# Adding the growing bank's states straight from PSUM in the down stage of a transformer layer

## The chip, the cores and the metric

The kernel runs on one core of one Trainium2 chip, in float32. The metric is the device time of one execution in microseconds (us). The engines are TensorE (PE, matmuls; PEld is its weight load), VectorE (DVE), ScalarE (ACT), GpSimd (POOL) and SyncE (SP, which issues the DMAs here). They run their own instruction streams in order and wait for one another by semaphores.

## What is computed

A layer with 2048 tokens (16 batches of 128) of width 1024: cross attention on a context, then a gated feed-forward net whose weights are 4-bit codes with scales for blocks of 64.

```python
x = x + xattn(layernorm(x), ctx, ctx)              # 8 heads
h = layernorm(x)
Wg, Wu, Wd = dequant_nf4(codes, scales)            # inner width I = 2752
inter = silu(h @ Wg.T) * (h @ Wu.T)                # 2048 x 2752
return x + inter @ Wd.T                            # 2048 x 1024: the down stage
```

## The kernel before

**Stages.** First a mixer stage (attention, up to some 180 us), then the gate and up products with the codes decoded beside them, to about 1101 us, and last the down stage, `inter @ Wd.T`, to the end. Float32 accuracy comes from splitting each operand into a high part (a cast to the matmul's rounded type) and a low part (operand less high part): each product is made of three matmuls, high by high, high by low and low by high.

**The down stage.** The inner dimension is cut into rounds of four blocks of 128 (`NR` = 5 rounds, r), the tokens into 8 pairs of tiles (`NM` = 8, m). One state g = 8r + m is one pair in one round: a 2 by 2 block product, made with 7 block products in place of 8 (the scheme of Strassen and Winograd). There are `NG` = 40 states. For a state the kernel needs the blocks of tokens themselves (`stage`, loaded by SyncE in `load_stage`, L421) and four sums S1 to S4 of them. The high parts are made by ScalarE (`hi_a`, L701, of three blocks, and `hi_s`, L707, of the four sums); VectorE makes the sums (`s_forms`, L903, four instructions of 256 columns in the tile `stemp`, shown at lines 910 and 846) and the low parts (`lo_a`, L899, 768 columns, and `lo_s`, L917, 1024 columns, both shown at line 846). The weights' forms were made in the earlier stage and are loaded once a round.

**The products of a state.** `product` (L1111) has six matmuls (128x128 by 128x512): two blocks of k, three parts each, shown at lines 1116 to 1118. The seven products 0 to 6 of a state go to three PSUM banks. Products 0, 2, 4 and 6 grow one bank, X: product 2 is accumulated onto product 0, and so on. Between them the growing sum has to be added to a part of the result. That is what the "s" adds are for: s1 takes X after product 0, s2 after product 2, s3 after product 4, and x after product 6. Products 1 and 5 grow the bank Q (adds q1 after product 1, q2 after product 5), product 3 the bank W (add w). The result `yacc` lies in SBUF with four parts of 128x512 for each pair (`part`, L932), and every add is `y = y + term` by VectorE, shown at line 930. Each finished product increments `product_done` by one, so a wait for `7g + k + 1` is a wait for product k of state g.

**How bank X is read.** ScalarE's `snapshot` (L713) copies bank X into one of two buffers `snap` as soon as the product is done (shown at line 717). TensorE waits only for that copy (`s1_ready`, `s2_ready`, `s3_ready`, L1150, L1158, L1166) and goes on with product 2, 4 or 6; VectorE adds from the copy later. The other adds, q1, q2, w and x, read PSUM directly, and TensorE waits for those of an older state or of product 1. `snap` lies over the two `inter` buffers of the stage before, so ScalarE waits for the last stores of `inter` ahead of its first copy (L735).

**The order on VectorE for a state g** (L986 to L1012): x_add(g-1), s1_add(g), s_forms(g+1), lo_a(g+1), q1_add(g), s2_add(g), w_add(g), lo_s(g+1), s3_add(g), q2_add(g). On ScalarE (L737 to L752): copy after product 0, hi_a(g+1), copy after product 2, hi_s(g+1), copy after product 4.

**The last round** (states 32 to 39) also has a rest: the inner width isn't a multiple of four blocks. After product 6 four groups of five matmuls (`rest`, lines 1125 to 1129) are added to the banks and to a bank Z, `rest_adds` (L968) takes the four adds, and a finished pair is stored. Its operands need a split too: `lo_rest` (L921) for each state, and once, in state 32, two subtractions for the weights (L1003 to L1006), all by VectorE.

Of the kernel before, what the change touches and what calls it, by code (L numbers as in the profile page):

```python
# [39 lines left out]
WIDE = 512  # L40
# [42 lines left out]
def wait(eng, sem, value):  # L83

    if not (isinstance(value, int) and value <= 0):
        eng.wait_ge(sem, value)


def xattn_ffn(nc, x, ctx, gu_codes, gu_scales, d_codes, d_scales, out):
    B, C, N = x.shape  # L90
# [8 lines left out]
    FULL = KT - 1  # L99
# [10 lines left out]
    NG = NR * NM  # L110
    KW = 4 * NR
    NP = 7
# [5 lines left out]
    with ExitStack() as st:  # L118
# [3 lines left out]
        def sem(name):  # L122
            return st.enter_context(nc.semaphore(name))
# [39 lines left out]
        def f(i, n=1):  # L163
            return F[:, i * N:(i + n) * N]
# [60 lines left out]
                 [R1[:, at_s + q * N:at_s + (q + 1) * N].rearrange("p (a n) -> p a n", a=2) for q in range(2)]]  # L225
        stage = [f(10), f(13)]
        stemp = f(11)
        snap = [F[:, 14 * N + i * WIDE:14 * N + (i + 1) * WIDE] for i in range(2)]
        blocks = [[stage[b][:, i * BK:(i + 1) * BK] for i in range(4)] for b in range(2)]
        S1, S2, S3, S4 = [stemp[:, i * BK:(i + 1) * BK] for i in range(4)]  # L230
        assert at_s + 2 * N == 2 * XW and at_a[0] + AB == 6 * ITEM
# [8 lines left out]
        bankX = [banks[0][:, 1, :], banks[3][:, 1, :]]  # L240
# [35 lines left out]
        inter_stored = [sem(f"inter_stored{s}") for s in range(2)]  # L276
# [4 lines left out]
        s_step, s_ready = sem("s_step"), sem("s_ready")  # L281
        ha_ready, la_ready, hs_ready, ls_ready = sem("ha_ready"), sem("la_ready"), sem("hs_ready"), sem("ls_ready")
        product_done = sem("product_done")
        s1_ready, s2_ready, s3_ready = sem("s1_ready"), sem("s2_ready"), sem("s3_ready")
        s1_added, s2_added, s3_added = sem("s1_added"), sem("s2_added"), sem("s3_added")
        q1_added, w_added, q2_added, x_added, z_added = [sem(n) for n in ("q1_added", "w_added", "q2_added", "x_added", "z_added")]
        restw_in, irest_in = sem("restw_in"), [sem(f"irest_in{b}") for b in range(2)]
# [298 lines left out]
        def _(act):  # L586
# [114 lines left out]
            def hi_a(g):  # L701

                act.wait_ge(stage_in[g % 2], 16 * (g // 2 + 1))
                wait(act, product_done, NP * (g - 2) + 6)
                nc.scalar.copy(aform[g % 2][0], stage[g % 2][:, 0:AB]).then_inc(ha_ready, 1)
# [4 lines left out]
                wait(act, product_done, NP * (g - 1))  # L710
                nc.scalar.copy(sform[g % 2][0], stemp.rearrange("p (a n) -> p a n", a=2)).then_inc(hs_ready, 1)

            def snapshot(g, i, product, freed, ready):  # L713

                act.wait_ge(product_done, NP * g + product + 1)
                wait(act, *freed)
                nc.scalar.copy(snap[i], bankX[g % 2]).then_inc(ready, 1)  # L717

            def hi_rest(m):

                act.wait_ge(irest_in[m % 2], 16 * (m // 2 + 1))
                wait(act, rest_done, 4 * (m - 1))
                if m == 0:
                    act.wait_ge(product_done, NP * (NG - NM))
                nc.scalar.copy(resti[m % 2][:, :, 0:2, :], irest[m % 2]).then_inc(hr_ready, 1)
# [6 lines left out]
            hi_s(0)  # L732
            last_block(2)
            last_block(3)
            for s in range(2):  # L735
                act.wait_ge(inter_stored[s], 16 * (2 * FULL + 4))
            for g in range(NG):  # L737
                r, m = g // NM, g % NM
                snapshot(g, 0, 0, (s3_added, g), s1_ready)
                if g + 1 < NG:  # L740
                    hi_a(g + 1)
                if r == NR - 1 and m == 0:
                    for k in range(2):
                        act.wait_ge(restw_in, 32)
                        nc.scalar.copy(restw[k][0], restw_in_f[k]).then_inc(hrw_ready, 1)
                    hi_rest(0)
                snapshot(g, 1, 2, (s2_added, g), s2_ready)
                if g + 1 < NG:
                    hi_s(g + 1)
                snapshot(g, 0, 4, (s1_added, g + 1), s3_ready)  # L750
                if r == NR - 1 and m + 1 < NM:
                    hi_rest(m + 1)  # L752

# [2 lines left out]
        def _(dve):  # L756
# [142 lines left out]
            def lo_a(g):  # L899
                dve.wait_ge(ha_ready, g + 1)  # L900
                sub(aform[g % 2][1], stage[g % 2][:, 0:AB], aform[g % 2][0].bitcast(F32)).then_inc(la_ready, 1)
# [15 lines left out]
            def lo_s(g):  # L917
                dve.wait_ge(hs_ready, g + 1)
                sub(sform[g % 2][1], stemp.rearrange("p (a n) -> p a n", a=2), sform[g % 2][0].bitcast(F32)).then_inc(ls_ready, 1)
# [9 lines left out]
            def add(y, term):  # L929
                return nc.vector.tensor_tensor(y, y, term, ALU.add)  # L930

            def part(g, t, h):  # L932
                return yacc[:, g % NM, t, h * WIDE:(h + 1) * WIDE]

            def s1_add(g):
                if g < NM:
                    dve.wait_ge(y_in[g], 16)
                dve.wait_ge(s1_ready, g + 1)
                add(part(g, 0, 0), snap[0]).then_inc(s1_added, 1)

            def q1_add(g):
                dve.wait_ge(product_done, NP * g + 2)
                add(part(g, 1, 1), bankQ[g % 2]).then_inc(q1_added, 1)

            def s2_add(g):
                dve.wait_ge(s2_ready, g + 1)
                add(part(g, 1, 0), snap[1]).then_inc(s2_added, 1)

            def s3_add(g):
                dve.wait_ge(s3_ready, g + 1)  # L950
                dve.wait_ge(q1_added, g + 1)
                add(part(g, 1, 1), snap[0]).then_inc(s3_added, 1)

            def w_add(g, done):
                dve.wait_ge(*done)
# [30 lines left out]
            for g in range(NG):  # L986
                r, m = g // NM, g % NM
                last = r == NR - 1
                if last and m:
                    rest_adds(g - 1)  # L990
                elif g:
                    x_add(g - 1, (product_done, NP * g))
                s1_add(g)
                if g + 1 < NG:
                    s_forms(g + 1)
                    lo_a(g + 1)
                q1_add(g)
                s2_add(g)
                if not last:
                    w_add(g, (product_done, NP * g + 4))  # L1000
                if g + 1 < NG:
                    lo_s(g + 1)
                if last and m == 0:  # L1003
                    for k in range(2):
                        dve.wait_ge(hrw_ready, k + 1)
                        sub(restw[k][1], restw_in_f[k], restw[k][0].bitcast(F32)).then_inc(lrw_ready, 1)  # L1006
                    lo_rest(0)
                s3_add(g)
                if not last:
                    q2_add(g, (product_done, NP * g + 6))  # L1010
                elif m + 1 < NM:
                    lo_rest(m + 1)  # L1012
# [4 lines left out]
        def _(pe):  # L1017
# [113 lines left out]
            for g in range(NG):  # L1131
                r, m, b = g // NM, g % NM, g % 2
                x, q, w2 = bankX[b], bankQ[b], bankW[b]
                a12, a11, a22 = [[aform[b][h][:, i * BK:(i + 1) * BK] for h in range(2)] for i in range(3)]
                s1, s2, s3, s4 = [[sform[b][h][:, i // 2, i % 2 * BK:(i % 2 + 1) * BK] for h in range(2)] for i in range(4)]
                in_place = 16 * (r + 1)

                pe.wait_ge(la_ready, g + 1)
                wait(pe, x_added, g - 1)
                if m == 0:  # L1140
                    pe.wait_ge(w_in[0], in_place)
                product(g, 0, x, a11, True)
                pe.wait_ge(ls_ready, g + 1)
                wait(pe, q2_added, g - 1)
                if g == 1:
                    pe.wait_ge(up_copied, 2)
                if m == 0:
                    pe.wait_ge(w_in[1], in_place)
                product(g, 1, q, s3, True)
                pe.wait_ge(s1_ready, g + 1)  # L1150
                if m == 0:
                    pe.wait_ge(w_in[2], in_place)
                product(g, 2, x, s2, False)
                wait(pe, w_added, g - 1)
                if m == 0:
                    pe.wait_ge(w_in[3], in_place)
                product(g, 3, w2, a12, True)
                pe.wait_ge(s2_ready, g + 1)  # L1158
                if m == 0:
                    pe.wait_ge(w_in[4], in_place)  # L1160
                product(g, 4, x, s1, False)
                pe.wait_ge(q1_added, g + 1)
                if m == 0:
                    pe.wait_ge(w_in[5], in_place)
                product(g, 5, q, a22, False)
                pe.wait_ge(s3_ready, g + 1)  # L1166
                if m == 0:
                    pe.wait_ge(w_in[6], in_place)
                product(g, 6, x, s4, False)
                if r == NR - 1:  # L1170
                    pe.wait_ge(lrw_ready, 2)
                    pe.wait_ge(lr_ready, m + 1)
                    if m == 0:
                        pe.wait_ge(up_copied, TB)
                    rest(m, w2, 0, 0, True)
                    rest(m, q, 1, 0, True)
                    rest(m, x, 0, 1, True)
                    wait(pe, z_added, m)
                    rest(m, bankZ, 1, 1, False)
# [46 lines left out]
```

## Time and profile before

| | |
|---|---|
| time, median of 3 runs | 1540.36 us (1540.14 to 1540.9) |
| the profiled execution: its time, its span | 1539.45 us, 1537.7 us |
| busy in the span: PE, PEld, DVE, ACT, POOL | 98%, 82%, 47%, 60%, 4% |
| DVE busy, ACT busy, in 1300 to 1350 us | 41.48 us, 18.75 us of 50 |
| mean granted clock of TensorE | 0.993 of full speed |

A line of a timeline gives the start in us, the duration in us, engine, line and operation, the tile written and the tiles read with their shapes, the count where like instructions are merged, and in brackets how long the engine was idle before and what released it. VectorE's and ScalarE's instructions overlap a little, so the distance between starts is less than the duration. A matmul is shown with its latency, 0.39 us, although the next one starts 0.23 us after it.

### The profile page before, as it was taken

The numbers are of one execution on the slowest core, as the hardware profiler recorded it, in microseconds if no ns is written. First come the engines' busy times: TensorE is split into PE (matmuls) and PEld (weight loads), VectorE is DVE, ScalarE is ACT, GpSimd is POOL, SyncE is SP. The second block draws the span as 40 slices with busy tenths as digits, with TensorE's granted clock in tenths as the row PEclk, the third lists the DMA queues.
The fourth block names the chain that finished last, engine by engine and source line by source line (L and its number), as shares of the span: only waits on it lengthen the run. The fifth ranks groups of instructions, "written<-read, shape, count | busy, mean of one in ns | idle before, by whom it ended". The sixth has DMA issues, their size and how long they took to land.

```text
span 1537.7 us, 18265 instructions
## 1 busy us (share of the span) xinstructions
PE 1509.7 (98%) x7056; PEld 1254.1 (82%) x7056; DVE 724.2 (47%) x1106; ACT 921.8 (60%) x1067; POOL 60.9 (4%) x99
## 2 busy tenths in 40 slices
PE   7999999999999999999999999999989999999998
PEld 6888788888888888888888888888768888888787
DVE  6998322322322222322322232222368888888764
ACT  6777876767677767676687767676223333333331
POOL 3343000000000000000000000000000000000000
PEclk9999999999999999999999999999999999999999
DMA  6554434444544454444443444436873535354332
GB/s 214 167 170 135 145 110 149 132 137 130 151 147 134 131 150 133 149 124 143 151 144 120 148 138 129 153 118 227 301 282 124 189 113 192 110 192 151 117 131 82
DMA packets 115462, 232.93 MB, mean 151 GB/s; under 512 B 8240, under 2 KB 55344, under 8 KB 110896
## 3 DMA queue, kind: packets, MB, share of 16 engines
q1 hardware_dynamic: 115376, 231.77, 46.9%
q8 instruction: 56, 0.92, 0.2%
q14 instruction: 30, 0.25, 0.1%
HBM read 154.14 MB, written 77.59 MB: 151 GB/s over the span
## 4 chain that ended last, share of the span: by engine, by line
PE 92%; ACT 4%; DMA 2%; issue 1%; DVE 1%; SPq 0%; DVEq 0%; POOL 0%; ACTq 0%
PE bank L1071 20%; PE bank L1069 20%; PE bank L1070 20%; PE bank L1116 8%; PE bank L1117 8%; PE bank L1118 8%; PE bank L1020 3%; PE bank L1047 1%; PE bank L1054 1%; DMA F<-inter_scratch 1%; PE bank L1037 1%; ACT early L602 1%; DMA inter_scratch<-F 1%; ACT F L615 1%; ACT F L636 1%
## 5 line engine op out<-in xcount | busy, mean ns | idle before, releaser
L1069 PE MATMUL bank<-R 128*128 128x512 f32 x1376 | 535.9, 389 | 0.0
L1070 PE MATMUL bank<-R 128*128 128x512 f32 x1376 | 535.7, 389 | 0.0
L1071 PE MATMUL bank<-R 128*128 128x512 f32 x1376 | 535.7, 389 | 0.0
L581 ACT ACTIVATE F<-F 128x1024 f32<-128x1024 f32 x441 | 467.6, 1060 | 13.3
L1070 PEld LDWEIGHTS bank<-R 128*128 128x128 f32 x1376 | 258.3, 188 | 53.7
L1071 PEld LDWEIGHTS bank<-R 128*128 128x128 f32 x1376 | 258.3, 188 | 53.6
L1069 PEld LDWEIGHTS bank<-R 128*128 128x128 f32 x1376 | 258.4, 188 | 53.3
L717 ACT COPY F<-bank 128x512 f32<-128x512 f32 x120 | 70.5, 587 | 271.0 <-PE bank L1118 267.1
L841 DVE TENSOR_TENSOR F<-F,bank 128x512 f32<-128x512 f32 x84 | 57.6, 686 | 331.1 <-issue 200.0
L648 ACT ACTIVATE F<-bank 128x512 f32<-128x512 f32 x84 | 49.8, 593 | 215.3 <-PE bank L1071 215.2
L767 DVE SCALAR_TENSOR_TENSOR F<-F 128x1024 f32<-128x1024 f32 x63 | 77.2, 1226 | 169.5 <-ACT F L581 169.5
L930 DVE TENSOR_TENSOR early<-early,bank 128x512 f32<-128x512 f32 x168 | 114.9, 684 | 36.0 <-PE bank L1129 23.9
L1118 PE MATMUL bank<-R 128*128 128x512 f32 x320 | 124.6, 389 | 0.0
L772 DVE TENSOR_TENSOR R<-F,R 128x1024 fp32r<-128x1024 f32 x41 | 50.2, 1225 | 154.9 <-ACT R L591 154.9
L846 DVE TENSOR_TENSOR F<-F 128x256 f32<-128x256 f32 (+2 forms) x230 | 121.0, 548 | 3.2 <-ACT F L661 1.1
L930 DVE TENSOR_TENSOR early<-early,F 128x512 f32<-128x512 f32 x120 | 82.6, 689 | 58.4 <-ACT F L717 57.9
L1118 PE MATMUL bank<-FR,R 128*128 128x512 f32 x240 | 94.6, 394 | 0.0
L1116 PE MATMUL bank<-R 128*128 128x512 f32 x232 | 90.6, 390 | 0.0
L1117 PE MATMUL bank<-R 128*128 128x512 f32 x232 | 90.5, 390 | 0.0
L1020 PE MATMUL bank<-ident,F 128*128 128x128 f32 x512 | 64.5, 279 | 9.9 <-DMA F<-in_ctx 5.8
L1116 PE MATMUL bank<-FR,R 128*128 128x512 f32 x168 | 66.5, 396 | 6.8 <-ACT F L717 6.8
L1118 PEld LDWEIGHTS bank<-R 128*128 128x128 f32 x320 | 60.2, 188 | 12.5
(92 smaller groups left out, 1479.2 us busy)
## 6 DMA issues: line engine op xcount, KB each, us to landing
wf_scratch<-F SPq DMA_DIRECT2D x70, 512.0 KB, 3.5
inter_scratch<-F SPq DMA_DIRECT2D x84, 256.0 KB, 2.3
F<-in_gu_codes SPq DMA_DIRECT2D x41, 512.0 KB, 5.0
F<-in_gu_scales SPq DMA_DIRECT2D x82, 256.0 KB, 4.2
F<-inter_scratch SPq DMA_DIRECT2D x40, 512.0 KB, 3.8
R<-wf_scratch SPq DMA_DIRECT2D x20, 1024.0 KB, 5.9
FR<-wf_scratch SPq DMA_DIRECT2D x15, 1024.0 KB, 5.9
F<-in_d_codes SPq DMA_DIRECT2D x22, 512.0 KB, 4.4
```

The costliest lines, as they stand in the source:

```text
L581: nc.scalar.activation(y, y, ACT.Prelu, bias=bias, scale=scale, alpha=alpha).then_inc(bent, 1)
L717: nc.scalar.copy(snap[i], bankX[g % 2]).then_inc(ready, 1)
L767: nc.vector.scalar_tensor_tensor(dst, level[s], ZERO, scales[s], ALU.add, ALU.mult).then_inc(w_ready, 1)
L846: return nc.vector.tensor_tensor(out, x, y, ALU.subtract)
L930: return nc.vector.tensor_tensor(y, y, term, ALU.add)
L1020: i = pe.transpose(dst[:, t * P:(t + 1) * P], src[:, t * P:(t + 1) * P], ident[:, :])
L1069: pe.matmul(dst, hi, xh[:, tb, t, :], start=(t == 0), stop=False)
L1070: pe.matmul(dst, hi, xl[:, tb, t, :], start=False, stop=False)
L1071: i = pe.matmul(dst, lo, xh[:, tb, t, :], start=False, stop=(t == HT - 1))
L1116: pe.matmul(dst, h, moving[:, 0, k, :], start=start and k == 0, stop=False, skip_group_check=not start)
L1117: pe.matmul(dst, h, moving[:, 1, k, :], start=False, stop=False, skip_group_check=not start)
L1118: last = pe.matmul(dst, l, moving[:, 0, k, :], start=False, stop=k == 1, skip_group_check=not start)
```

## The change

ScalarE's three copies a state, their buffers and their semaphores go, and with them its wait for the last stores of `inter`. VectorE's s1_add, s2_add and s3_add wait for the product itself and read bank X from PSUM, and TensorE waits for these adds (`s1_added`, `s2_added`, `s3_added`) where it waited for the copies. The order on VectorE becomes: x_add(g-1), s1_add, q1_add, s_forms(g+1), s2_add, w_add, lo_a(g+1), s3_add, lo_s(g+1), q2_add. The four sums are made by VectorE before and after. In state 32 the two subtractions of weights and the first lo_rest stand between lo_a and s3_add.

```diff
@@ ScalarE
-            def snapshot(g, i, product, freed, ready):
-                act.wait_ge(product_done, NP * g + product + 1)
-                wait(act, *freed)
-                nc.scalar.copy(snap[i], bankX[g % 2]).then_inc(ready, 1)
...
-            for s in range(2):
-                act.wait_ge(inter_stored[s], 16 * (2 * FULL + 4))
             for g in range(NG):
                 r, m = g // NM, g % NM
-                snapshot(g, 0, 0, (s3_added, g), s1_ready)
+                act.wait_ge(product_done, NP * g + 1)
                 if g + 1 < NG:
                     hi_a(g + 1)
...
-                snapshot(g, 1, 2, (s2_added, g), s2_ready)
                 if g + 1 < NG:
                     hi_s(g + 1)
-                snapshot(g, 0, 4, (s1_added, g + 1), s3_ready)
@@ VectorE
-                dve.wait_ge(s1_ready, g + 1)
-                add(part(g, 0, 0), snap[0]).then_inc(s1_added, 1)
+                dve.wait_ge(product_done, NP * g + 1)
+                add(part(g, 0, 0), bankX[g % 2]).then_inc(s1_added, 1)
...
-                dve.wait_ge(s2_ready, g + 1)
-                add(part(g, 1, 0), snap[1]).then_inc(s2_added, 1)
+                dve.wait_ge(product_done, NP * g + 3)
+                add(part(g, 1, 0), bankX[g % 2]).then_inc(s2_added, 1)
...
-                dve.wait_ge(s3_ready, g + 1)
+                dve.wait_ge(product_done, NP * g + 5)
                 dve.wait_ge(q1_added, g + 1)
-                add(part(g, 1, 1), snap[0]).then_inc(s3_added, 1)
+                add(part(g, 1, 1), bankX[g % 2]).then_inc(s3_added, 1)
...
                 s1_add(g)
+                q1_add(g)
                 if g + 1 < NG:
                     s_forms(g + 1)
-                    lo_a(g + 1)
-                q1_add(g)
                 s2_add(g)
                 if not last:
                     w_add(g, (product_done, NP * g + 4))
                 if g + 1 < NG:
-                    lo_s(g + 1)
+                    lo_a(g + 1)
                 if last and m == 0:
...
                     lo_rest(0)
                 s3_add(g)
+                if g + 1 < NG:
+                    lo_s(g + 1)
@@ TensorE
-                pe.wait_ge(s1_ready, g + 1)
+                pe.wait_ge(s1_added, g + 1)
...
-                pe.wait_ge(s2_ready, g + 1)
+                pe.wait_ge(s2_added, g + 1)
...
-                pe.wait_ge(s3_ready, g + 1)
+                pe.wait_ge(s3_added, g + 1)
```

## Rows read from the trace of the kernel before

**Rows 1.** The page, busy us (share of the span) and instructions of TensorE.

```profile
PE 1509.7 (98%) x7056; PEld 1254.1 (82%) x7056; DVE 724.2 (47%) x1106; ACT 921.8 (60%) x1067; POOL 60.9 (4%) x99
```

**Rows 2.** TensorE's waits, 850 to 1540 us: total us, times, longest.

```profile
PE bank L1116 <- ACT F L717: 10.0, 3, 6.8
PE bank L1125 <- DVE R L846: 0.9, 1, 0.9
```

**Rows 3.** Groups by line and shape, 1100 to 1540 us: busy us, mean ns, idle before.

```profile
L930 DVE TENSOR_TENSOR early<-early,bank 128x512 f32<-128x512 f32 x168 | 114.9, 684 | 36.0 <-PE bank L1129 23.9 <-PE bank L1118 11.9
...
L930 DVE TENSOR_TENSOR early<-early,F 128x512 f32<-128x512 f32 x120 | 82.6, 689 | 58.4 <-ACT F L717 57.9
L717 ACT COPY F<-bank 128x512 f32<-128x512 f32 x120 | 70.5, 587 | 271.0 <-PE bank L1118 267.1 <-DMA inter_scratch<-F 3.9
```

**Rows 4.** Timeline of VectorE in state 20, with the next state's first add.

```profile
1305.48 0.69 DVE L930 TENSOR_TENSOR early<-early,bank 128x512 f32<-128x512 f32 x1 [0.38 <-PE bank L1118]
1307.46 0.69 DVE L930 TENSOR_TENSOR early<-early,F 128x512 f32<-128x512 f32 x1 [1.29 <-ACT F L717]
1308.07 0.42 DVE L910 TENSOR_TENSOR F<-F 128x256 f32<-128x256 f32 x1
1308.40 1.22 DVE L846 TENSOR_TENSOR F<-F 128x256 f32<-128x256 f32 x3
1309.53 0.95 DVE L846 TENSOR_TENSOR R<-F,R 128x768 fp32r<-128x768 f32 x1
1310.40 0.68 DVE L930 TENSOR_TENSOR early<-early,bank 128x512 f32<-128x512 f32 x1
1311.00 0.69 DVE L930 TENSOR_TENSOR early<-early,F 128x512 f32<-128x512 f32 x1
...
1312.20 1.22 DVE L846 TENSOR_TENSOR R<-F,R 128x1024 fp32r<-128x1024 f32 x1
...
1315.00 0.69 DVE L930 TENSOR_TENSOR early<-early,bank 128x512 f32<-128x512 f32 x1 [0.38 <-PE bank L1118]
```

**Rows 5.** Timeline of TensorE, state 20: first matmuls of products 0 and 1.

```profile
1305.28 0.39 PE L1116 MATMUL bank<-FR,R 128*128 128x512 f32 x1
...
1306.64 0.39 PE L1116 MATMUL bank<-FR 128*128 128x512 f32 x1
```

**Rows 6.** Timeline in state 32: product 4 waits for a copy.

```profile
1424.73 0.39 PE L1118 MATMUL bank<-FR,R 128*128 128x512 f32 x1
1425.35 0.50 PE L1116 MATMUL bank<-FR 128*128 128x512 f32 x1 [0.23 <-ACT F L717]
...
1424.71 0.58 ACT L717 COPY F<-bank 128x512 f32<-128x512 f32 x1
```

**Rows 7.** Timeline around the load of state 2's blocks: SyncE, VectorE, ScalarE, TensorE.

```profile
1108.88 1.67 SPq L428 DMA_DIRECT2D F<-inter_scratch  x1
...
1126.68 0.43 DVE L910 TENSOR_TENSOR F<-F 128x256 f32<-128x256 f32 x1 [8.07 <-DMA F<-inter_scratch]
...
1127.42 0.58 ACT L717 COPY F<-bank 128x512 f32<-128x512 f32 x1
...
1128.05 0.79 PE L1116 MATMUL bank<-FR,R 128*128 128x512 f32 x1 [6.77 <-ACT F L717]
1128.64 0.63 PE L1117 MATMUL bank<-FR,R 128*128 128x512 f32 x1
```

**Rows 8.** Timeline of state 32: VectorE's low parts and the rest's first matmul.

```profile
1427.42 3.12 DVE L846 TENSOR_TENSOR R<-R 128x1024 fp32r<-128x1024 f32 x4
...
1430.64 0.47 PE L1125 MATMUL bank<-R 128*128 128x512 f32 x1 [0.92 <-DVE R L846]
```

**Rows 9.** Windows: us, PE PEld DVE ACT POOL busy, granted clock, DMA share, GB/s.

```profile
80.00:120.00 40.00, 39.18 (x289) 33.76 (x288) 37.04 (x67) 32.05 (x40) 16.37 (x22) 0.96 0.54 165
1420.00:1436.00 16.00, 14.85 (x65) 11.70 (x64) 12.99 (x21) 6.27 (x9) 0.00 (x0) 1.00 0.18 54
```

**Rows 10.** Timeline of VectorE's sums for state 0 and ScalarE's cast behind them.

```profile
1092.52 1.21 DVE L846 TENSOR_TENSOR F<-F 128x256 f32<-128x256 f32 x3
...
1093.82 1.05 ACT L711 CAST FR<-F 128x1024 fp32r<-128x1024 f32 x1 [2.34 <-DVE F L846]
```

More of the change, by code:

```diff
@@ L227, in xattn_ffn @@
         stemp = f(11)
-        snap = [F[:, 14 * N + i * WIDE:14 * N + (i + 1) * WIDE] for i in range(2)]
         blocks = [[stage[b][:, i * BK:(i + 1) * BK] for i in range(4)] for b in range(2)]
@@ L283, in xattn_ffn @@
         product_done = sem("product_done")
-        s1_ready, s2_ready, s3_ready = sem("s1_ready"), sem("s2_ready"), sem("s3_ready")
         s1_added, s2_added, s3_added = sem("s1_added"), sem("s2_added"), sem("s3_added")
```

## The prediction

> **What bounds the kernel now.** I read the page's busy table first: TensorE is busy for 1509.7 of 1537.7 us [rows 1], and the reader is to see in it that only idle time of TensorE, or work added to it, can move the time much. The change lies in the down stage, from about 1101 us to the end, so the second view is the list of TensorE's waits in that part [rows 2]: 10.0 us on ScalarE's copies (three waits) and 0.9 us on VectorE. There is nothing else to win. The third view, instructions grouped by line, gives the stage's load outside TensorE [rows 3]: 120 copies by ScalarE, 120 adds from the copies and 168 adds straight from PSUM by VectorE. The fourth and fifth are the timelines of VectorE and TensorE in one undisturbed state, g = 20 [rows 4, 5]. There TensorE starts a matmul every 0.227 us, so a product (six of them) takes 1.36 us (1305.28 to 1306.64) [rows 5], and a state's seven take 9.52 us, which is also the distance of VectorE's like adds (1305.48 and 1315.00) [rows 4]. TensorE doesn't wait in such a state.
>
> I count time t from the first matmul of product 0 of a state. Product k then begins at 1.36k, that is at 0, 1.36, 2.72, 4.08, 5.44, 6.80, 8.16, and the next state at 9.52. Two turnarounds are needed:
> - TensorE to VectorE: the add of the old state's product 6 starts at 1305.48, 0.20 after the next product's first matmul at 1305.28 [rows 4, 5]. So a product's result can be read 0.20 after the boundary.
> - another engine to TensorE: a ScalarE copy ends at 1425.29 and the waiting matmul, shown at 1425.35 with 0.50 instead of 0.39 us, really runs from 1425.46: 0.17 [rows 6]. From VectorE: subtractions end at 1430.54, the matmul shown at 1430.64 with 0.47 runs from 1430.72: 0.18 [rows 8]. Some 0.02 more is lost on the matmuls behind it [rows 6], so 0.20 in all.
>
> VectorE's instructions overlap by some 0.09, so I cost them by start to start: an add 0.60 [rows 4] (1310.40 to 1311.00), the four sums of blocks 1.46 (1308.07 to 1309.53), the low part of the first blocks (lo_a) 0.87 (1309.53 to 1310.40), the low part of the sums (lo_s) 1.13 (1.22 less the overlap). An add's own result stands 0.69 after its start.
>
> **Removed: the copies.** 120 copies of 0.59 us leave ScalarE [rows 3], which idles before them for PE: worth nothing by itself. VectorE's adds cost the same from either source, 684 and 689 ns [rows 3], so VectorE gains and loses nothing in busy time. The four sums are VectorE's in both kernels; the diff only moves them, whatever its few words say.
>
> The VectorE page of the Trainium skill (VectorE: DVE Perf Modes, the section on the TRN2 errata) speaks against the change: it gives an access from PSUM 62 cycles more than one from SBUF, which I estimate as 0.065 us for each add. The trace disagrees: 684 ns from PSUM, 689 from SBUF [rows 3]. By the Trainium skill the sum below would be 36 times 0.065, or 2.3 us, higher.
>
> **Moved: who releases products 2, 4 and 6.** Before, the release is a copy, which starts as soon as the product ends and never stands behind VectorE's other work. After, it is an add in VectorE's queue, in the order of the diff. I go through that queue in a state:
> - x_add of the old state starts at 0.20.
> - s1_add waits for product 0: it starts at 1.36 + 0.20 = 1.56, ends at 2.25, and product 2 could go on at 2.45. It is due at 2.72: hidden, with 0.3 to spare.
> - q1_add waits for product 1: 2.72 + 0.20 = 2.92.
> - The four sums follow 0.60 later, at 3.52, and hold VectorE until 4.98. Product 2 ended meanwhile, and s2_add could have read it from 4.28.
> - s2_add starts at 4.98, ends at 5.67, and product 4 goes on at 5.67 + 0.20 = 5.87. It was due at 5.44. **TensorE stands for 0.42 us** (0.43 by these sums; rounding goes both ways).
> - w_add at 5.64 (product 3 wasn't delayed), lo_a at 6.24, and s3_add, which waits for the delayed product 4, at 5.86 + 1.36 + 0.20 = 7.42. It ends at 8.11; product 6, now due at 8.58, could go on at 8.31: hidden.
> - lo_s at 8.02 to 9.15, q2_add at 9.15, and VectorE is free at 9.75, ahead of 9.94 + 0.20 for the next x_add. So nothing adds up from state to state, and the period becomes 9.52 + 0.42 = 9.94.
>
> Queued behind the s2_add wait are w_add, lo_a and s3_add, all with room; lo_a ends at 7.2 instead of about 5.2, and behind it SyncE loads the blocks of two states later. Those are wanted a whole state later, some 16 us, so no price. ScalarE's casts keep ready times ahead of VectorE's need for them.
>
> The wait falls into every state that makes sums for a successor. States 0 and 1 and state 32 are special (below), state 39 makes none, so 36 states pay: 36 x 0.42 = **15.1 us**.
>
> **The start of the stage.** Before, ScalarE's first copy waited for the last stores of inter, since the copy's buffer lay over theirs, and TensorE stood for 3.0 us (10.0 less 6.8 and 0.2) [rows 2, 6]. That wait goes. What is late next is the load of the blocks of state 2, which lands at 1126.68 whatever the engines do: it was issued at 1108.88 behind other loads [rows 7]. Before, a cast and a copy follow (the copy from 1127.42 to 1128.00), and product 4 of state 1 goes on at 1128.05, after the 6.8 us wait [rows 2, 7]. After, the sums stand between the load and s2_add: 1126.68 + 1.46 + 0.69 + 0.18 = 1129.01, against 1128.21 (the shown start plus the first matmul's extra 0.16). That's **0.8 us** later, and the 3.0 us won before it are waited away here. Likewise in state 0, where the sums for state 1 need blocks from the same queue.
>
> **State 32.** With the last round VectorE also makes four low parts for the rest, which hold it for 3.15 us (start 1427.42, end 1430.54) [rows 8]. Before, they delay only the rest: it runs from 1430.72 instead of 1429.56, 1.16 late, and product 4 was 0.5 late (1425.46 for 1424.96) [rows 6, 8]. After, they stand before s3_add: 4.98 + 0.60 + 0.87 + 3.15 = 9.60, its end 10.29, product 6 at 10.48 instead of 8.58: 1.9 us, with 0.42 before it, and the rest then finds its operands ready. 2.32 less the 1.69 that go: **+0.6 us**. In states 33 to 38 only the 0.42 returns, already counted.
>
> **Sum.** 15.1 + 0.8 + 0.6 = 16.5 us on the profiled execution's 1539.45 gives 1555.95; on the median of 1540.36 it gives 1556.9. The two differ by 0.9 us, under the range.
>
> **Bounds of the 0.42.** Below: if the sums ran at the 0.33 from start to start of their first pair (1308.07 to 1308.40), they'd take 1.34 and the stall is 0.30: 1540.4 + 1.4 + 10.8 = 1552.6. Above: nothing in the trace shows an add that releases a product, so the turnaround might be 0.1 longer: 0.52, 1560.5. I take the measured middle, since both turnarounds I have (0.17, 0.18) agree.
>
> **Rivals.**
> 1. *The stall is hidden, not slower.* Product 4 is released in time if s2_add starts by 4.55, that is, if the four sums take 1.03 instead of 1.46 us, for instance because ScalarE no longer works beside them. Then only the ends count: 1540.4 + 1.4 = 1541.8. Against it: for state 0 ScalarE stood idle until 1093.82, and the last three sums took 1.21 us, as against 1.22 in an undisturbed state [rows 4, 10]. Chance 0.05 (with some of it for a gain at the start, if the loads land earlier: 3 us less, 1537.4).
> 2. *Three stalls a state.* s1_add and s3_add have only 0.3 to spare. If an add releases 0.4 later than I reckon, product 4 stands for 0.8 and the other two for 0.1 each: 36 x 1.0 + 1.4 = 37 us, 1578. The 0.18 of [rows 8] speaks against it. Chance 0.05.
> 3. *TensorE's clock falls.* After the 6.8 us wait the matmuls start 0.43 apart instead of 0.227 (1128.21 to 1128.64) [rows 7], the lower of the two levels, and such a dip costs about 8 x 0.2 = 1.6 us. One for each stall would be 58 us more: 1615. For it: at 80 to 120 us, where TensorE works on small tiles with short gaps, the granted clock is 0.96; against it, it is 1.00 over 1420 to 1436, gaps of 0.5 and 1.2 us included [rows 9]. The TensorE page of the Trainium skill (TensorE: Matmul & The Clock Gate, the section on a second failure mode) tells of such a fall from very short idle times between groups of matmuls. Chance 0.03.
>
> **How the numbers follow.** My forecast has 0.87: 1556.9. The range, 1552 to 1562, takes in both bounds of the stall and about 1.5 us for a dip more or less at the start; beyond it lie the rivals and some of my own case. This kernel's measurement can tell about 0.2%, or 3.1 us, from no change. Faster 0.02, the same 0.05 (rival 1), slower 0.93.
>
> **What would show it.** In the profile after: TensorE's waits name VectorE's L-line of the adds, some 38 times at about 0.15 us shown idle each (a 0.42 delay shows as less, since the matmul before it ends 0.16 after the boundary and the first one's extra 0.11 is hidden in its length); like adds 9.94 apart; ScalarE's busy time 70 us less; VectorE's unchanged; one wait of about 1.6 us near state 32; the wait in state 1 about 0.8 longer. Wrong would be: periods of 9.52 (rival 1), waits at products 2 and 6 (rival 2), a granted clock below 0.99 in the undisturbed stretch (rival 3), or a first wait whose end moves.

## The result and the profile after

The changed kernel takes 1558.45 us (median of 4 runs, 1557.0 to 1558.91) against 1540.63 us before (1540.14 to 1542.16): a ratio of 1.0112, 95% interval 1.0095 to 1.013. It is slower by 17.8 us; 16.5 had been forecast. The profiled execution took 1558.91 us, with a span of 1557.2. Its line numbers differ: an add is L918 (L930 before), the sums L898 and L834, a product's matmuls L1105 to L1107.

The busy table and TensorE's waits from 850 us on (total us, times, longest), to be read against [rows 1, 2]:

```profile
PE 1520.6 (98%) x7056; PEld 1252.0 (80%) x7056; DVE 731.3 (47%) x1106; ACT 858.9 (55%) x947; POOL 60.8 (4%) x99
...
PE bank L1105 <- DVE early L918: 11.6, 4, 5.7
```

This list shows four waits, and 11.6 us where there had been 10.9: it doesn't explain 18 us. "PE" even has more busy time than before. The reason is that a matmul is shown with its latency: the last matmul of a product reaches 0.16 us past the moment at which the next product is due and so covers part of a wait of 0.4, and the late matmul is itself shown 0.11 longer. The row of the weight loads (PEld) has no such cover. Its waits in the undisturbed stretch, 1140 to 1420 us:

```profile
PEld bank L1105 <- DVE early L918: 15.4, 28, 0.6
```

28 waits in 280 us, one for each state, at 0.55 us each. (Part of each 0.55 is there without a stall as well, since a weight load takes 0.19 of the 0.23 between two.) The same stretch in windows, first of before and then of after (us, busy and count of PE, PEld, DVE, ACT, POOL, granted clock, DMA share, GB/s):

```profile
1140.00:1420.00 280.00, 280.00 (x1237) 231.95 (x1237) 230.27 (x383) 100.46 (x146) 0.00 (x0) 1.00 0.45 156
```

```profile
1140.00:1420.00 280.00, 276.39 (x1184) 219.75 (x1183) 226.30 (x367) 52.86 (x56) 0.00 (x0) 1.00 0.41 147
```

What tells most is the count: 1184 matmuls in place of 1237, that is 4.3% fewer in the same time (a period of 9.52 x 1.045 = 9.95 us), at a granted clock of 1.00 in both.

VectorE in one undisturbed state (19), to be read against [rows 4]; its first matmul starts at 1306.34:

```profile
1306.55 0.69 DVE L918 TENSOR_TENSOR early<-early,bank 128x512 f32<-128x512 f32 x1 [0.30 <-PE bank L1107]
1307.90 0.69 DVE L918 TENSOR_TENSOR early<-early,bank 128x512 f32<-128x512 f32 x1 [0.67 <-PE bank L1107]
1309.26 0.69 DVE L918 TENSOR_TENSOR early<-early,bank 128x512 f32<-128x512 f32 x1 [0.67 <-PE bank L1107]
1309.87 0.42 DVE L898 TENSOR_TENSOR F<-F 128x256 f32<-128x256 f32 x1
1310.20 1.22 DVE L834 TENSOR_TENSOR F<-F 128x256 f32<-128x256 f32 x3
1311.34 1.33 DVE L918 TENSOR_TENSOR early<-early,bank 128x512 f32<-128x512 f32 x2
1312.59 0.95 DVE L834 TENSOR_TENSOR R<-F,R 128x768 fp32r<-128x768 f32 x1
1313.76 0.69 DVE L918 TENSOR_TENSOR early<-early,bank 128x512 f32<-128x512 f32 x1 [0.23 <-PE bank L1107]
...
1316.50 0.69 DVE L918 TENSOR_TENSOR early<-early,bank 128x512 f32<-128x512 f32 x1 [0.32 <-PE bank L1107]
```

The rows are x_add, s1, q1, the sums, s2 and w merged, lo_a, s3, and x_add of the next state 9.95 us later. Counted from the first matmul they lie at 0.21, 1.56, 2.92, 3.53, 5.00, 6.25 and 7.42. And TensorE at product 4:

```profile
1311.56 0.39 PE L1107 MATMUL bank<-FR,R 128*128 128x512 f32 x1
1312.08 0.50 PE L1105 MATMUL bank<-FR,R 128*128 128x512 f32 x1
```

The first matmul of product 4 was due at 1311.78 and, with its extra 0.11, really runs from 1312.19: 0.41 us late. The list of idle times shows nothing in brackets for it, as the gap on the row is 0.13 us.

**Where the 19.4 us between the two spans lie** (19.5 by the rounded spans), each from the distance of like instructions in the two traces:

| stretch | later by |
|---|---|
| before the down stage (first matmul 1100.96, after 1102.42), same code | 1.46 |
| to the start of state 2 | 1.83 |
| states 2 to 31 (285.60 and 298.49 us for 30 states, 0.43 each) | 12.89 |
| state 32 (15.74 and 16.41) | 0.67 |
| states 33 to 38, and the last (98.38 and 100.95) | 2.57 |
| from the last add (1533.84 and 1553.26) to the end | 0.00 |

The first 1.46 us stand there before any changed code has run. Without them the two executions lie 18.0 us apart, close to the 17.8 of the medians.

At the start of the stage TensorE's waits moved. Before, they were 3.01 us ahead of product 2 of state 0 and 6.77 ahead of product 4 of state 1. After, there are 0.28 at product 2 of state 0, 3.97 at product 4 of state 0 and 5.72 at product 4 of state 1:

```profile
1112.83 0.80 PE L1105 MATMUL bank<-FR 128*128 128x512 f32 x1 [3.97 <-DVE early L918]
...
1130.92 0.79 PE L1105 MATMUL bank<-FR,R 128*128 128x512 f32 x1 [5.72 <-DVE early L918]
```

### The profile page after: what moved, and what is told of

It is laid out like the page before. It is cut to its first block, busy times and chain, and to the rows that moved or that the text cites. A ratio compares the mean times of both kernels' runs of the same rounds, so it can differ in the third digit from the quotient of the medians.

```text
span 1557.2 us, 18028 instructions
## 1 busy us (share of the span) xinstructions
PE 1520.6 (98%) x7056; PEld 1252.0 (80%) x7056; DVE 731.3 (47%) x1106; ACT 858.9 (55%) x947; POOL 60.8 (4%) x99
## 4 chain that ended last, share of the span: by engine, by line
PE 84%; DVE 6%; ACT 3%; issue 3%; DMA 3%; SPq 0%; DVEq 0%; ACTq 0%
PE bank L1058 20%; PE bank L1060 20%; PE bank L1059 20%; PE bank L1105 6%; PE bank L1107 6%; PE bank L1106 6%; PE bank L1009 2%; DVE early L918 2%; DVE F L834 2%; DMA F<-inter_scratch 1%; DVE F L898 1%; PE bank L1026 1%; ACT early L600 1%; PE bank L1043 1%; PE bank L1036 1%
## 5 line engine op out<-in xcount | busy, mean ns | idle before, releaser
L918 DVE TENSOR_TENSOR early<-early,bank 128x512 f32<-128x512 f32 x288 | 196.1, 685 | 104.5 <-PE bank L1107 82.0
L703 ACT CAST R<-F 128x768 fp32r<-128x768 f32 x40 | 33.6, 840 | 247.8 <-PE bank L1107 226.0
L1107 PE MATMUL bank<-R 128*128 128x512 f32 x320 | 125.4, 392 | 0.0
L834 DVE TENSOR_TENSOR F<-F 128x256 f32<-128x256 f32 (+2 forms) x230 | 121.1, 548 | 3.2 <-ACT F L659 1.1
L1107 PE MATMUL bank<-FR,R 128*128 128x512 f32 x240 | 94.4, 394 | 0.0
L1105 PE MATMUL bank<-R 128*128 128x512 f32 x232 | 92.3, 398 | 1.0
L1105 PE MATMUL bank<-FR,R 128*128 128x512 f32 x168 | 67.2, 400 | 7.0 <-DVE early L918 5.7
L1009 PEld LDWEIGHTS bank<-ident,F 128*128 128x128 f32 x512 | 60.1, 148 | 15.1 <-issue 14.3
L1107 PEld LDWEIGHTS bank<-R 128*128 128x128 f32 x320 | 60.5, 189 | 13.2
```

Source lines behind the costliest of these rows:

```text
L834: return nc.vector.tensor_tensor(out, x, y, ALU.subtract)
L1009: i = pe.transpose(dst[:, t * P:(t + 1) * P], src[:, t * P:(t + 1) * P], ident[:, :])
L1105: pe.matmul(dst, h, moving[:, 0, k, :], start=start and k == 0, stop=False, skip_group_check=not start)
L1107: last = pe.matmul(dst, l, moving[:, 0, k, :], start=False, stop=k == 1, skip_group_check=not start)
```

## The experiments

The theory: product 4 of each state waits because s2_add stands behind the four sums, which themselves stand behind an add that can't start earlier. The rivals: an add is a worse release than a copy wherever it stands; or the new order is bad in itself.

**Sums before q1_add.** The changed kernel with

```diff
                 s1_add(g)
-                q1_add(g)
                 if g + 1 < NG:
                     s_forms(g + 1)
+                q1_add(g)
                 s2_add(g)
```

> The changed kernel, with one edit: VectorE makes the four sums before q1_add instead of behind it. Theory (the sums' place between q1_add and s2_add is what holds product 4): VectorE can start the sums 0.6 us after s1_add, at 2.16 of the state, is done with q1_add at 4.22, and s2_add starts at 4.28 when product 2 is done; a state takes 9.52 us again, the short wait at product 4 is gone, and the time is about 1542.5 us (1540.6 plus the later end of the wait in state 1). Rival A (reading the bank directly is slower by itself, whatever the order): the period stays near 9.95, about 1558. Rival B (more work between load and s2_add only costs at the start): same as the theory.

Measured: 1542.35 us against 1540.81 of the kernel before, ratio 1.0009 (0.9999 to 1.0018). Its timeline of VectorE, the same part of a state:

```profile
1308.94 0.69 DVE L918 TENSOR_TENSOR early<-early,bank 128x512 f32<-128x512 f32 x1 [0.67 <-PE bank L1107]
1309.55 0.42 DVE L898 TENSOR_TENSOR F<-F 128x256 f32<-128x256 f32 x1
1309.88 1.22 DVE L834 TENSOR_TENSOR F<-F 128x256 f32<-128x256 f32 x3
1311.02 1.33 DVE L918 TENSOR_TENSOR early<-early,bank 128x512 f32<-128x512 f32 x2
1313.03 0.69 DVE L918 TENSOR_TENSOR early<-early,bank 128x512 f32<-128x512 f32 x1 [0.67 <-PE bank L1107]
...
1318.46 0.69 DVE L918 TENSOR_TENSOR early<-early,bank 128x512 f32<-128x512 f32 x1 [0.67 <-PE bank L1107]
```

The sums now fill the time in which VectorE waited for product 1, q1 and s2 follow (merged, the second with product 2), and the next s1_add is 9.52 us away. One call moved gives back 16 of the 18 us. In the undisturbed states the add as such costs nothing as a release; rival A falls. What is left of the difference, within the noise of this comparison, lies at the start in the traces: state 2 begins 34.9 us after the stage's first matmul, against 33.0 in the kernel before.

**The new order with the copies kept.** The kernel before, its loop on VectorE replaced by that of the changed one; ScalarE and TensorE untouched.

> The kernel before, with ScalarE's copies kept, but with the changed kernel's order of VectorE's work. Theory: TensorE waits only for ScalarE's copies, so the order costs nothing: period 9.52 us, about 1540.5 us. Rival (the new order is bad by itself, through lo_a or lo_s coming later): well over 1550.

Measured: 1540.37 us, ratio 0.9995 (0.9985 to 1.0004). TensorE's period is 9.52 us in every undisturbed state. So the new order costs nothing while TensorE waits only for ScalarE. The loss needs both: a release that stands in VectorE's queue, and work ahead of it there. What the adds cost without the new order is the next experiment.

**The old order with adds from PSUM.** The changed kernel with

```diff
                 s1_add(g)
-                q1_add(g)
                 if g + 1 < NG:
                     s_forms(g + 1)
+                    lo_a(g + 1)
+                q1_add(g)
                 s2_add(g)
                 if not last:
                     w_add(g, (product_done, NP * g + 4))
                 if g + 1 < NG:
-                    lo_a(g + 1)
+                    lo_s(g + 1)
...
                 s3_add(g)
-                if g + 1 < NG:
-                    lo_s(g + 1)
```

> The changed kernel's adds straight from PSUM, but in the order of VectorE's work before the change: s1_add, sums, lo_a, q1_add, s2_add, w_add, lo_s, s3_add. Theory: s2_add stands behind 1.46 + 0.87 + 0.60 us of other work after s1_add and starts at 5.09, so product 4 goes on at 5.98 instead of 5.44: 0.54 us in each of 36 states (19.4), 1.0 in state 32, and the wait in state 1 ends 1.5 us later than in the changed kernel; about 1564 us, period 10.06. Rival A (the adds themselves cost it, not their place): as the changed kernel, 1558.

Measured: 1565.4 us, ratio 1.016 (1.0144 to 1.0175), 24.6 us over before. Its timeline of VectorE, s1, sums, lo_a, and q1, s2 and w in one row, then the next s1:

```profile
1301.10 0.69 DVE L918 TENSOR_TENSOR early<-early,bank 128x512 f32<-128x512 f32 x1 [0.67 <-PE bank L1106]
1301.70 0.42 DVE L898 TENSOR_TENSOR F<-F 128x256 f32<-128x256 f32 x1
1302.04 1.22 DVE L834 TENSOR_TENSOR F<-F 128x256 f32<-128x256 f32 x3
1303.17 0.95 DVE L834 TENSOR_TENSOR R<-F,R 128x768 fp32r<-128x768 f32 x1
1304.04 1.88 DVE L918 TENSOR_TENSOR early<-early,bank 128x512 f32<-128x512 f32 x3
...
1311.19 0.69 DVE L918 TENSOR_TENSOR early<-early,bank 128x512 f32<-128x512 f32 x1 [0.67 <-PE bank L1106]
```

A period of 10.09, 0.57 over 9.52, where 0.54 had been worked out. The adds alone, in the old order, thus cost more than the whole change. The diff's reordering was a help, but it left the sums on the wrong side of q1_add.

**One sum before q1_add, three behind.** `s_forms` is cut after its first instruction (S1), and the rest, `s_forms_rest`, is called after q1_add:

```diff
                 s1_add(g)
+                if g + 1 < NG:
+                    s_forms(g + 1)
                 q1_add(g)
                 if g + 1 < NG:
-                    s_forms(g + 1)
+                    s_forms_rest(g + 1)
                 s2_add(g)
```

> The changed kernel, with the first of the four sums before q1_add and three behind it: the dose between none and four. Theory: s2_add starts 0.33 us earlier, at 4.65, product 4 goes on at 5.54 instead of 5.44: 0.1 us in each of 36 states, 3.6 in all; about 1546.5 us, period 9.62. Rival A: 1558.

Measured: 1545.37 us, ratio 1.0029 (1.0018 to 1.004). Its s1_adds in three states that follow one another:

```profile
1301.24 0.69 DVE L921 TENSOR_TENSOR early<-early,bank 128x512 f32<-128x512 f32 x1 [0.67 <-PE bank L1113]
...
1310.82 0.69 DVE L921 TENSOR_TENSOR early<-early,bank 128x512 f32<-128x512 f32 x1 [0.67 <-PE bank L1113]
...
1320.44 0.69 DVE L921 TENSOR_TENSOR early<-early,bank 128x512 f32<-128x512 f32 x1 [0.67 <-PE bank L1113]
```

The periods take turns at 9.58 and 9.62 us, 9.60 in the mean over states 2 to 31. So a state stalls for 0.08, where 0.1 had been expected. By the theory product 4 is in time if s2_add starts by 4.55 of the state. It starts at 4.28 with the sums first, at 4.65 with three sums behind q1_add, at 4.98 with four, and at 5.09 in the old order. The stalls measured are 0, 0.08, 0.43 and 0.57 us. The step from three to four is 0.35, about the 0.34 us that a sum costs; with the sums first all is hidden. The cost has a threshold, as the theory has it.

**The start of the stage.** Four kernels look at the other term of the sum, the last of them with all the edits together. First, with the sums before q1_add, the work for the next state at the end of VectorE's order in states 0 and 1:

```diff
                 s1_add(g)
-                if g + 1 < NG:
+                if 2 <= g < NG - 1:
                     s_forms(g + 1)
...
-                if g + 1 < NG:
+                if 2 <= g < NG - 1:
                     lo_a(g + 1)
                 s3_add(g)
-                if g + 1 < NG:
+                if 2 <= g < NG - 1:
                     lo_s(g + 1)
                 if not last:
                     q2_add(g, (product_done, NP * g + 6))
+                if g < 2:
+                    s_forms(g + 1)
+                    lo_a(g + 1)
+                    lo_s(g + 1)
```

> The kernel with the sums first (the swap that gave 1542.4 us), with one more edit: in states 0 and 1 the sums and low parts for the next state, which need the late loads, come at the end of VectorE's order instead of ahead of q1_add and s2_add. Theory (at the start TensorE stands because s2_add is queued behind sums that wait for a load): product 4 of states 0 and 1 no longer waits; TensorE waits instead ahead of states 1 (some 2 us) and 2 (some 7 us, till about 2.5 us after the load has landed), one fall of the clock in place of two; about 1538 us. Rival (the load's landing alone sets when state 2 begins, wherever the sums stand): no gain, 1542.

Measured: 1537.85 us, ratio 0.9979 (0.9969 to 0.9988). TensorE's waits at the start are those that were expected, 1.76 us before state 1 and 6.6 before state 2:

```profile
1113.09 0.51 PE L1109 MATMUL bank<-FR,R 128*128 128x512 f32 x1 [1.76 <-DVE R L834]
1129.56 0.80 PE L1109 MATMUL bank<-FR,R 128*128 128x512 f32 x1 [6.56 <-DVE R L834]
```

Second, again with the sums before q1_add, the loads of the result's parts for pairs 2 to 7 put into SyncE's loop:

```diff
-            for m in range(NM // 4, NM):
-                load_y(m)
...
                 if g + 2 < NG:
                     load_stage(g + 2)
+                if g + 2 < NM:
+                    load_y(g + 2)
```

> The kernel with the sums first, with one more edit: the loads of the result's parts for pairs 2 to 7 are issued one for each state instead of all ahead of the blocks of state 2. Theory (state 2's blocks land at 1127 because 6 MB stand before them in the queue): they land near 1110, the wait of 6.1 us in state 1 is gone with its fall of the clock, the wait in state 0 stays; about 1534 us. Rival (the load is slow for another reason): 1542.

Measured: 1533.97 us, ratio 0.9954 (0.9939 to 0.9969). The wait in state 1 is gone; the one in state 0 (4.66 us) stays. Third, the same edit of the loads in the kernel before:

> The kernel before, with ScalarE's copies, and the same edit of the loads. Theory: the 6.8 us wait in state 1 goes, with its fall of the clock (1.6 us); the 3 us wait of the first copy for the stores stays; about 1532 us, so the copies are about 2 us ahead of the adds from PSUM at the start, since only ScalarE's cast and copy stand behind the load of state 1. Rival: 1541.

Measured: 1531.26 us, ratio 0.9935 (0.992 to 0.995). The wait for state 2's blocks was one of place in the queue, in both kernels. With the copies the kernel is 2.7 us ahead of the adds by the medians. The traces put 1.7 of it into state 0 (15.9 us with the copies, 17.7 with the adds), where ScalarE's cast and copy are a shorter way from the load of state 1 to product 4 than VectorE's sums and two adds. The rest has no place in the down stage that the traces show.

Fourth, all of it together (adds from PSUM, with the later loads of the second experiment), and in state 32 only one subtraction of weights ahead of s3_add, the other and lo_rest behind it:

```diff
                 s1_add(g)
-                q1_add(g)
-                if g + 1 < NG:
+                if 1 <= g < NG - 1:
                     s_forms(g + 1)
+                q1_add(g)
...
-                if g + 1 < NG:
+                if 1 <= g < NG - 1:
                     lo_a(g + 1)
                 if last and m == 0:
-                    for k in range(2):
-                        dve.wait_ge(hrw_ready, k + 1)
-                        sub(restw[k][1], ...).then_inc(lrw_ready, 1)
-                    lo_rest(0)
+                    dve.wait_ge(hrw_ready, 1)
+                    sub(restw[0][1], ...).then_inc(lrw_ready, 1)
                 s3_add(g)
+                if last and m == 0:
+                    dve.wait_ge(hrw_ready, 2)
+                    sub(restw[1][1], ...).then_inc(lrw_ready, 1)
+                    lo_rest(0)
+                if g == 0:
+                    s_forms(1)
+                    lo_a(1)
```

> The adds from PSUM with everything that the traces point to: sums before q1_add, the later loads of the result, in state 0 the sums and lo_a behind s3_add, and in state 32 one subtraction of weights before s3_add and the other with lo_rest behind it. Theory: no wait over 1.5 us is left in the down stage and the clock doesn't fall there; state 2 starts some 12 us earlier than before, the 1.7 us in state 32 go; about 1527 us. Rival (the loads can't keep up once state 1 begins earlier): 1532 or more.

Measured: 1526.41 us (1525.89 to 1527.21), ratio to the kernel before 0.9905 (0.9889 to 0.9922). Against the kernel before, state 2 begins 11.7 us earlier in the trace, and state 32 takes 1.4 us less. The only wait that TensorE's list has for the down stage, and the windows, which show the granted clock at 1.00 from the first state on (before, it was 0.87 from 1100 to 1140):

```profile
PE bank L1110 <- DVE R L834: 0.4, 1, 0.4
```

```profile
1100.00:1140.00 40.00, 39.48 (x171) 31.46 (x171) 31.57 (x52) 8.73 (x10) 0.00 (x0) 1.00 0.79 294
1140.00:1400.00 260.00, 260.00 (x1149) 215.29 (x1148) 216.46 (x355) 51.28 (x55) 0.00 (x0) 1.00 0.46 162
```

**What the adds are worth in that kernel.** The same with ScalarE's copies back, and in state 0 `hi_a(1)` and `hi_s(1)` behind ScalarE's third copy.

> The best kernel so far (1526.4 us) with ScalarE's copies put back: same order on VectorE, same loads, same places in states 0 and 32, and ScalarE's casts for state 1 behind its copies of state 0. It tells what the adds straight from PSUM are worth once nothing else holds TensorE. Theory: in an undisturbed state nothing (period 9.52 either way); at the start the first copy waits again for the last stores of inter, product 2 of state 0 stands some 3 us and the clock falls for 1.6 us; state 1 begins about 4 us later: about 1530 us. Rival A (the copies release TensorE sooner and are worth something in each state): 1526 or less. Rival B (the first copy's wait is hidden by the load for state 1, which TensorE must await anyway): 1526.5.

Measured: 1532.29 us (1530.38 to 1534.29), ratio 0.994 (0.9923 to 0.9956). The copies are 5.9 us behind the adds by the medians. The two profiled executions lie 7.9 apart: 0.4 ahead of the down stage, 6.1 to the start of state 2, 1.4 in state 32, and nothing in the undisturbed states (9.52 in both). TensorE's waits, at the start and in state 32:

```profile
1108.07 0.79 PE L1125 MATMUL bank<-FR 128*128 128x512 f32 x1 [2.86 <-ACT F L717]
1119.00 0.50 PE L1125 MATMUL bank<-FR,R 128*128 128x512 f32 x1 [1.00 <-DVE R L849]
...
1420.16 0.50 PE L1125 MATMUL bank<-FR 128*128 128x512 f32 x1 [0.23 <-ACT F L717]
...
1425.45 0.47 PE L1134 MATMUL bank<-R 128*128 128x512 f32 x1 [0.91 <-DVE R L849]
```

From the first matmul of state 0 to that of state 1 it is 17.1 us here (1102.05 to 1119.11) and 10.5 in the kernel with the adds (1101.63 to 1112.11). That is the wait for the stores, the fall of the clock behind it (14 matmuls at the lower level, where eight had been reckoned) and a wait for lo_a. The wait for the stores comes from the place of the copy's buffer over `inter`, not from the copying; this is read from the code and the trace, as a buffer elsewhere wasn't tried. The wait for lo_a comes with this kernel's own order: `hi_a(1)` stands behind the third copy. In the kernel with copies and only the later loads, where it stands ahead, the same distance is 15.9 us, and that kernel is no slower in all (1531.26). Against it the adds are worth 4.9 us.

In state 32 the copy after product 2 stands behind ScalarE's casts of the rest's weights. It starts at 1419.53, 5.20 us into the state, where the product could be read at 4.28. So a copy, too, is a late release when its engine has work queued ahead of it.

## Why the prediction was right

**The stall of 0.42 us: right.** The adds stand within 0.02 us of the times worked out for them (0.21, 1.56, 2.92, 3.53, 5.00, 6.25 and 7.42 for 0.20, 1.56, 2.92, 3.52, 4.98, 6.24 and 7.42), and a state takes 9.95 us for 9.94. 36 states gave 15.5 us (12.89 and 2.57) for 15.1. The rows on which it rested were the starts, not the durations, of VectorE's instructions in an undisturbed state, and two turnarounds. The bounds (0.30 to 0.52) weren't needed. That the place of the sums in the queue of the releasing engine does it is shown by the first four experiments: moved ahead of q1_add they cost nothing, with the copies they cost nothing in either place, and in the two other places the stall is as long as the queue makes it.

**The Trainium skill** (VectorE: DVE Perf Modes, the section on the TRN2 errata) would have put 2.3 us on it, and the trace disagrees. Adds from PSUM took 685 ns in the changed kernel too, where all 288 are of this kind, and the places above leave no room for 0.065 us more on each.

**The start: mechanism right, size off.** Forecast 0.8 us, measured 1.83 by the start of state 2. The way from the landed load to product 4 is as it was reckoned: 1128.72 to 1131.08, 2.36 us for 2.33, and that part is the forecast's 0.8. What was missed are two terms that the prediction took as fixed. The load landed 26.3 us after the stage's first matmul instead of 25.7 (0.58 later). In the five other kernels with the same loads it is 26.4 to 26.5 in four, one of them with the copies, and 25.7 in one, with the adds. And TensorE's lower clock behind the wait lasted longer: from the wait's end to state 2 it took 6.13 instead of 5.71 (0.42). Of four other kernels with this wait, three took 5.5 and one 6.6. Both terms thus vary among kernels in a way that doesn't go by copies or adds, so I take them for scatter and not for an effect of the change; one trace of each kernel can't show it. The remark that a dip more or less may cost 1.5 us covered them.

One sign failed here: the wait in state 1 was to be about 0.8 us longer, and it is 1.05 shorter (5.72 for 6.77). What was to be some 0.8 later is the end of the wait, which the load sets. The prediction named the queue behind the load in state 0 but gave it no price. TensorE stands 3.97 us there and then runs 12 matmuls at the lower clock, where there had been 8 in state 0, so it comes later to product 4 of state 1 and waits less for it.

**State 32: right.** 0.67 us for 0.6, with one shown wait of 1.62 at product 6, where 1.6 had been expected. (The low parts there hold VectorE for 3.12 us by the row, not 3.15; it changes nothing.)

**What is left** is 1.46 us before the down stage, where the code is the same. In the eleven traces of this study the down stage's first matmul starts between 1100.66 and 1102.92 us, with no change to anything ahead of it, so I take this part for scatter of single executions; there is one trace of each kernel. The forecast of 16.5 us is to be held against the 18.0 without it.

**The rivals.** A hidden stall asked for sums in 1.03 us; they took 1.47. Three stalls a state: product 2 and 6 were on time, the queue behind s2_add had the room that was worked out. The clock: 1.00 over the whole undisturbed stretch with a stall of 0.41 every 9.95 us, and 1.00 as well in the old order with its longer stalls. The Trainium skill (TensorE: Matmul & The Clock Gate, the section on a second failure mode) tells of a clock that falls from very short idle times; no run here shows it in the down stage.

**What the prediction got wrong was where to look.** It expected 38 short waits in TensorE's list, and the list has four in all; the short ones stand with the weight loads. It expected VectorE's busy time unchanged and ScalarE's less by 70 us; they moved by +7.1 and -62.9. A likely reason is that an instruction's duration includes some 0.09 us that it shares with a neighbour, while work that stands alone is counted in full; this wasn't worked through.

## What to carry to other kernels

When a release moves from one engine to another, look less at the instruction than at what stands ahead of it in the new engine's queue between the moment that its data is ready and the moment that it is due. Write down these two times for each release and the free stretches between them, and put movable work (here the sums) into a stretch before an add that has to wait anyway: the same work cost 0.43 us a state behind q1_add and nothing before it. A load that lands late holds all that is queued behind its first user, so look first at what stands ahead of it in the DMA queue: moving six loads was worth 9.5 us to the kernel before.

## What the hardware showed beyond that

- A stall of 0.41 us leaves 0.13 us on the matmul row, and no entry in TensorE's list of waits, but 0.55 us on the weight-load row. The stalls of 0.57 in the old order do stand in the list: 41 waits, 23.8 us in all.
- The time at the lower clock behind a long wait varied: 8 matmuls at 0.43 us from start to start after the 6.8 us wait of the kernel before, 14 (the last at 0.40) after a wait of 2.9 us in the last experiment. In the kernel with no wait over 1 us in the down stage the granted clock was 1.00 from its first window on.
- Where product 4 came only 0.06 to 0.10 us late, with three sums behind q1_add, its first matmul is shown with 0.45 us, not with the 0.50 of the longer stalls. That part of the weight load is still hidden then would fit, but isn't shown.
